# A DLRM kernel on one core: half of W1 loaded behind the first gather, and the feature units of chunks 0 and 1 dealt out anew

## The chip, the cores and the metric

One core of a Trainium2 chip runs the whole program. The metric is the device time of one execution in microseconds; lower is better.

## The reference

For each of 2048 samples there are 27 feature vectors of 128 floats and one dense vector of 128. The dot products of all 351 pairs of feature vectors, behind the dense vector, are the input of a perceptron of four ReLU layers and a last row:

```python
dots = jnp.einsum('bfd,bgd->bfg', bottom_output, bottom_output)
pairs = dots[:, _TRIL_I, _TRIL_J]
x = jnp.concatenate([bottom_mlp_output, pairs, pad], axis=1)      # 2048 x 480
for w, b in ((w0, b0), (w1, b1), (w2, b2), (w3, b3)):             # 1024, 1024, 512, 256
    x = jax.nn.relu(x @ w.T + b)
return x @ w_out.T + b_out                                        # 2048 x 1
```

All is float32. The kernel splits each operand into a high and a low part, so that one product of layers takes three matmuls.

## The kernel before, in words

**Chunks and units.** The batch is cut into 8 chunks of 256 samples (columns). The features of a chunk are handled in 16 units of 16 samples. A unit takes these steps: SP loads its rows in four DMAs (`load_rows`, L458); DVE transposes them (`turn_raw`, L921, "raw"); ACT makes the high part of the result (L805) and DVE the low one (L926), both into `xt`; PE forms the products of the features (`gram`, four matmuls of 256 columns, L688); ACT moves them to `parts` (four instructions, L817); DVE transposes the low part (L945, `low_t`) and POOL adds twice (L564, L571) into `grams`. When all 16 units of a chunk are in `grams`, SP writes them to DRAM (`spill`, L405, `blocks<-grams`) and reads them back with pairs on partitions (`gather`, L410, `pairs<-blocks`); ACT and DVE split them into `x0` (L843, L980). That is the input of the next chunk's layer 0.

**Layers.** A tile of a layer is 128 outputs by 256 columns, with K steps of three matmuls each (L726). Layers 0, 1, 2, 3 have 8, 8, 4, 2 tiles of K = 4, 8, 8, 4: 96, 192, 96 and 24 matmuls, 408 in a chunk. A finished tile is drained by ACT (L833), its high part cast by DVE (L952), its low part made by POOL (L579), and the next layer waits for that on its first tile. In layer 3 the fourth K step of both tiles, nine matmuls with what goes before it, comes last (`LAST_LAYER`), as it needs layer 2's last tile.

**Order of the work.** Every engine walks the same list of steps (`steps_of`), so its queue is fixed. Steps of other work are hooked in between the matmuls: in chunk 0 a hook every 6 matmuls (`first_hooks`), in later chunks every 18 (`hooks_of`). Hook n of a chunk's units (`unit_steps`) holds raw of unit n, the xt of unit n-1, and the gram of unit n-3; so 19 hooks do 16 units. The first five hooks of a chunk's units (`AHEAD`) are placed near the end of the chunk before the one that has the rest; with them five raws and two grams. Before: chunk 0 has all 19 hooks for the features of chunk 1 (places 11 to 37 of its hooks) and at places 49 to 61 the first five for chunk 2. Chunk 1 and the later ones have 14 hooks (every 18 matmuls, the last after 252), two empty ones, and the five for the chunk after.

**SP's queue in chunk c.** `load_mlp`, rows of chunk c+1 from unit 9, rows of units 0 to 3 of chunk c+2, spill, gather, and only then rows of units 4 to 8 of chunk c+2.

**The start.** The features of chunk 0 go another way: PE turns the rows (L647), ACT copies (L790), PE multiplies (L671), ACT moves one quarter of the result (L798) and DVE three (L935). Then the weights are turned by PE in groups of four 128x128 tiles (L642, or L621 for the small vectors), ACT makes the high part (L782, L780) and DVE the low (L912, or `ones`, L909). Groups 0 to 7 are W0, 8 the small vectors, 9 to 24 W1, 25 to 34 W2 and W3. ACT issues half of the first spill and of the first gather from its own queue; the gather stands behind group 6 (`GATHER_AFTER`) and waits there for the spill. The pair columns of x are K steps 1 to 3 of layer 0; step 0 (the dense vector) of the first six tiles is done ahead of them (`EARLY_TILES`), and W1's groups 9 on are hooked in between, one every six matmuls.

## Time and profile before

| what | value |
|---|---|
| median of 3 runs | 532.54 us (530.84 to 533.41) |
| the profiled execution, its own time | 532.41 us |
| its span | 530.6 us |
| PE busy | 501.3 us (94%) |
| ACT, DVE, POOL busy | 333.7, 289.1, 260.6 us |
| mean granted TensorE clock | 0.988 |

The profiled execution's time is its span and 1.8 us around it. The engines' busy times overlap, so they don't add up to the span. The granted clock is 1.00 at 2.4 GHz and 0.50 at 1.2 GHz.

### The profile page before, as it was taken

The numbers are of one execution on the slowest core, as the hardware profiler recorded it, in microseconds if no ns is written. First come the engines' busy times: TensorE is split into PE (matmuls) and PEld (weight loads), VectorE is DVE, ScalarE is ACT, GpSimd is POOL, SyncE is SP. The second block draws the span as 40 slices with busy tenths as digits, with TensorE's granted clock in tenths as the row PEclk, the third lists the DMA queues.
The fourth block names the chain that finished last, engine by engine and source line by source line (L and its number), as shares of the span: only waits on it lengthen the run. The fifth ranks groups of instructions, "written<-read, shape, count | busy, mean of one in ns | idle before, by whom it ended". The sixth has DMA issues, their size and how long they took to land.

```text
span 530.6 us, 13442 instructions
## 1 busy us (share of the span) xinstructions
PE 501.3 (94%) x4073; PEld 491.5 (93%) x4073; DVE 289.1 (54%) x646; ACT 333.7 (63%) x844; POOL 260.6 (49%) x467
## 2 busy tenths in 40 slices
PE   6968987799999999999999999999999999999996
PEld 6858987699999899999999999999999999999996
DVE  3764877466753576446762676356753676232101
ACT  4644799747974588737883698657873698433112
POOL 2800356424865267634864287625764387524221
PEclk9996999999999999999999999999999999999999
DMA  8997677644563566356663656266653662210000
GB/s 246 264 312 156 196 119 114 114 77 81 89 109 75 94 105 104 55 109 113 102 96 67 116 96 106 44 125 109 99 79 79 117 103 43 49 47 1 1 1 0
DMA packets 281054, 53.23 MB, mean 100 GB/s; under 512 B 265126, under 2 KB 279230, under 8 KB 281022
## 3 DMA queue, kind: packets, MB, share of 16 engines
q1 hardware_dynamic: 279090, 52.22, 51.9%
q10 hardware_dynamic: 1932, 0.61, 0.5%
q8 instruction: 17, 0.28, 0.2%
q14 instruction: 15, 0.12, 0.1%
HBM read 45.71 MB, written 7.09 MB: 99 GB/s over the span
## 4 chain that ended last, share of the span: by engine, by line
PE 66%; DMA 11%; SPq 7%; ACT 5%; POOL 4%; issue 4%; DVE 3%; POOLq 0%; DVEq 0%; ACTq 0%
PE acc L726 52%; PE gram_ps L688 8%; DMA blocks<-grams 5%; ACT parts L817 3%; SPq L410 3%; DMA early_rows<-in_r_bottom_output_dram 2%; SPq L405 2%; PE gram_ps L642 2%; DMA rows<-in_r_bottom_output_dram 2%; PE gram_ps L671 2%; POOL grams L571 1%; SPq L458 1%; POOL h_a L579 1%; POOL parts L564 1%; DMA pairs<-blocks 1%
## 5 line engine op out<-in xcount | busy, mean ns | idle before, releaser
L726 PE MATMUL acc<-h_a,w_hi 128*128 128x256 f32 x1152 | 214.4, 285 | 3.9 <-POOL h_a L579 2.6
L726 PEld LDWEIGHTS acc<-h_a,w_hi 128*128 128x128 f32 x1152 | 179.1, 192 | 6.6 <-POOL h_a L579 4.3
L817 ACT ACTIVATE parts<-gram_ps 27x216 f32<-27x216 f32 x448 | 152.9, 341 | 25.7 <-PE gram_ps L688 18.5
L833 ACT ACTIVATE h_full<-acc,small_t 128x256 f32<-128x256 f32 x172 | 81.5, 474 | 132.2 <-PE acc L726 128.7
L726 PE MATMUL acc<-h_a,w_lo 128*128 128x256 f32 x576 | 162.8, 283 | 0.0
L579 POOL TENSOR_TENSOR h_a<-h_full,h_a 128x256 fp32r<-128x256 f32 x96 | 72.2, 752 | 139.6 <-DVE h_a L952 139.6
L726 PEld LDWEIGHTS acc<-h_a,w_lo 128*128 128x128 f32 x576 | 110.3, 192 | 0.0
L726 PE MATMUL acc<-h_b,w_hi 128*128 128x256 f32 x512 | 93.9, 284 | 0.0
L726 PE MATMUL acc<-x,w_hi 128*128 128x256 f32 x480 | 90.7, 288 | 0.0
L579 POOL TENSOR_TENSOR h_b<-h_full,h_b 128x256 fp32r<-128x256 f32 x64 | 47.4, 740 | 83.1 <-DVE h_b L952 83.1
L564 POOL TENSOR_TENSOR parts<-parts 128x128 f32<-128x128 f32 x112 | 82.4, 736 | 6.1 <-ACT parts L817 5.5
L926 DVE TENSOR_TENSOR xt<-raw,xt 128x432 fp32r<-128x432 f32 x112 | 82.0, 732 | 4.2 <-ACT xt L805 4.2
L921 DVE STREAM_TRANSPOSE raw<-rows 128x512 f32<-128x512 f32 x112 | 78.4, 700 | 6.2 <-DMA rows<-in_r_bottom_output_dram 6.0
L726 PEld LDWEIGHTS acc<-h_b,w_hi 128*128 128x128 f32 x512 | 79.7, 192 | 0.0
L688 PE MATMUL gram_ps<-xt 128*128 128x256 f32 x448 | 72.9, 285 | 6.3 <-ACT parts L817 5.9
L726 PEld LDWEIGHTS acc<-x,w_hi 128*128 128x128 f32 x480 | 75.5, 194 | 1.4 <-issue 0.8
L952 DVE CAST h_a<-h_full 128x256 fp32r<-128x256 f32 x96 | 32.2, 336 | 80.1 <-ACT h_full L833 80.1
L726 PE MATMUL acc<-h_b,w_lo 128*128 128x256 f32 x256 | 72.4, 283 | 0.0
L688 PEld LDWEIGHTS gram_ps<-xt 128*128 128x128 f32 x448 | 61.6, 192 | 8.8 <-DVE xt L926 4.4
L952 DVE CAST h_b<-h_full 128x256 fp32r<-128x256 f32 x64 | 18.8, 294 | 93.2 <-ACT h_full L833 93.2
L726 PE MATMUL acc<-x,w_lo 128*128 128x256 f32 x240 | 68.3, 285 | 0.0
L805 ACT ACTIVATE xt<-raw 128x432 fp32r<-128x432 f32 x112 | 62.5, 558 | 1.8 <-DVE raw L921 1.4
(59 smaller groups left out, 439.5 us busy)
## 6 DMA issues: line engine op xcount, KB each, us to landing
rows<-in_r_bottom_output_dram SPq DMA_DIRECT2D x444, 64.0 KB, 2.1
blocks<-grams SPq DMA_DIRECT2D x30, 216.0 KB, 3.9
w_raw<-in_L_rec_w_dram SPq DMA_DIRECT2D x6, 1024.0 KB, 7.9
early_rows<-in_r_bottom_output_dram SPq DMA_DIRECT2D x12, 224.0 KB, 5.7
stage_pairs<-in_L_rec_w_dram SPq DMA_DIRECT2D x1, 1408.0 KB, 9.2
w_raw<-in_L_rec_w_dram SPq DMA_DIRECT2D x2, 512.0 KB, 8.5
mlp_rows<-r_bottom_mlp_output_dram SPq DMA_DIRECT2D x8, 128.0 KB, 2.2
pairs<-blocks SPq DMA_DIRECT2D x8, 126.0 KB
```

What stands on the lines that cost most here:

```text
L405: engine.dma_start(blocks[:, :, s * RUN:(s + 1) * RUN], grams[QUAD * s:QUAD * (s + 1)]).then_inc(spilled, 16)
L410: engine.dma_start(pairs[q % P:q % P + nf * nk, q // P], src).then_inc(gathered[q // P], 16)
L564: nc.gpsimd.tensor_tensor(hh, hh, hl, ALU.add).then_inc(sum_done, 1)
L579: nc.gpsimd.tensor_tensor(h[:, m, 1, :], h_full[:, slot % 2, :], h[:, m, 0, :].bitcast(F32), ALU.subtract).then_inc(split_done, 1)
L688: last = nc.tensor.matmul(gram_ps[:, u % GRAM_RING * GRAM_BANKS + j // 2, at:at + 2 * P], xt[:, u % XT_RING, j, 0], xt[:, u % XT_RING, j]. ...
L726: last = nc.tensor.matmul(acc_slot(c, slot), weight(wp, layer, m, k), in_tile(layer, k, xp), start=(k == 0 and n == 0), stop=(k == K_TILES ...
L805: nc.scalar.activation(xt_part(u, 0), raw_cols(u), ACT.Copy).then_inc(xt_hi_done, 1)
L817: last = nc.scalar.activation(parts[quad_of(s), u % 2, :, :, 0:FEATS], gram_found(u, s), ACT.Copy)
L833: nc.scalar.activation(h_full[:, slot % 2, :], acc_slot(c, slot), ACT.Relu, bias=small_t[:, slot:slot + 1]).then_inc(drained, 1)
L921: nc.vector.transpose(raw[:, u % RAW_RING].rearrange("p j n -> p (j n)"), rows[:, r].rearrange("p j n -> p (j n)")).then_inc(raw_turned, 1)
L926: nc.vector.tensor_tensor(xt_part(u, 1), raw_cols(u), xt_part(u, 0).bitcast(F32), ALU.subtract).then_inc(xt_done, 1)
L952: nc.vector.tensor_copy(h[:, m, 0, :], h_full[:, slot % 2, :]).then_inc(high_done, 1)
```

## The change

Six things, all of which move instructions in queues; none adds or takes away arithmetic.

1. SP loads rows 4 to 7 of W1 (two DMAs of 1 MB) behind its part of the first gather. Before, one of the two stood ahead of the spill and one between spill and gather.
2. The moving of the last two units of chunk 0 is split two quarters to two between ACT and DVE (one to three before), and each of weight groups 0 to 3 on PE waits only for the unit that had its bank.
3. `GATHER_AFTER` goes from 6 to 3: ACT's half of the gather stands behind group 3.
4. All six early K steps are done in a row, then groups 9 to 11 of W1, and only then ACT and DVE split the pairs. The memset of `xt` on DVE (L1017) is thereby ahead of groups 9 to 11.
5. Chunk 0 has only the 19 hooks for chunk 1, at places 10 to 40, each place now 18 matmuls later than before as the early steps aren't counted; W2's and W3's groups follow from place 41.
6. Chunk 1 is written out, with a hook every 15 matmuls: 19 for chunk 2, the last after 285 matmuls, and right behind them the five for chunk 3. From chunk 2 on all is as before.

```diff
--- before.py
+++ after.py
@@ -57,14 +57,14 @@
-HOOK, FIRST_HOOK = 18, 6
-GATHER_AFTER, FIRST_UNIT, LATE_HOOK = 6, 11, 38
-AHEAD, AHEAD_HOOK = 5, 49
+HOOK, SECOND_HOOK, FIRST_HOOK = 18, 15, 6
+GATHER_AFTER, W1_EARLY, FIRST_UNIT, LATE_HOOK = 3, 3, 10, 41
+AHEAD = 5
 FULL_ROWS = 112
 EARLY_SLOTS = 8
 RAW_RING = 2
 EARLY_XT = 2 * XT_RING
-EARLY_BY_ACT = 1
+EARLY_BY_ACT = [1] * (UNITS - 2) + [2] * 2
 OUT_HOOK, EARLY_TILES = 2, 6
@@ -146,43 +146,40 @@
         steps.append(("weights", n))
         if n == GATHER_AFTER:
             steps.append(("gather",))
-    return steps + [("pairs",)]
+    return steps
 def first_hooks():
-    places = [FIRST_UNIT + 2 * i for i in range(4)] + [FIRST_UNIT + 8 + 4 * i // 3 for i in range(UNIT_HOOKS - 4)]
-    hooks = [[] for _ in range(3 * sum(K_TILES[n] * M_TILES[n] for n in range(3)) // FIRST_HOOK)]
-    for n in range(BEFORE_CHUNK, LATE_WEIGHTS):
-        hooks[n - BEFORE_CHUNK].append(("weights", n))
-    for u, place in enumerate(places):
-        hooks[place] += unit_steps(u, 1)
+    hooks = [[] for _ in range(3 * TILE0[3] // FIRST_HOOK)]
+    for n in range(BEFORE_CHUNK + W1_EARLY, LATE_WEIGHTS):
+        hooks[n - BEFORE_CHUNK - W1_EARLY].append(("weights", n))
+    for u in range(UNIT_HOOKS):
+        hooks[FIRST_UNIT + 5 * u // 3] += unit_steps(u, 1)
+    assert FIRST_UNIT + 5 * (UNIT_HOOKS - 1) // 3 < LATE_HOOK
     for n in range(LATE_WEIGHTS, W_GROUPS):
         hooks[LATE_HOOK + n - LATE_WEIGHTS].append(("weights", n))
-    assert places[-1] < LATE_HOOK
-    for n in range(AHEAD):
-        hooks[AHEAD_HOOK + 3 * n] += unit_steps(n, 2)
     return hooks
-def hooks_of(now, ahead):
-
-
-
-    hooks = [unit_steps(n, 1) for n in range(AHEAD, UNIT_HOOKS)] if now else []
+def hooks_of(now, ahead, begun, every):
+
+
+
+    hooks = [unit_steps(n, 1) for n in range(begun, UNIT_HOOKS)] if now else []
     if ahead:
-        hooks += [[] for _ in range(len(hooks), 3 * TILE0[2] // HOOK)] + [unit_steps(n, 2) for n in range(AHEAD)]
+        hooks += [[] for _ in range(len(hooks), 3 * TILE0[2] // every)] + [unit_steps(n, 2) for n in range(AHEAD)]
     return hooks
-def chunk_steps(now, ahead, first):
+def chunk_steps(now, ahead, first, second):
     steps, done = [], 0
-    hooks = first_hooks() if first else hooks_of(now, ahead)
-    every = FIRST_HOOK if first else HOOK
+    every = FIRST_HOOK if first else SECOND_HOOK if second else HOOK
+    hooks = first_hooks() if first else hooks_of(now, ahead, 0 if second else AHEAD, every)
     hooks.reverse()
     def products(layer, m, k, k1):
@@ -200,8 +197,8 @@
                 steps.append(("out",))
     if first:
-        for m in range(EARLY_TILES):
-            products(0, m, 0, 1)
+        steps += [("mm", 0, m, 0, 1) for m in range(EARLY_TILES)]
+        steps += [("weights", BEFORE_CHUNK + n) for n in range(W1_EARLY)] + [("pairs", 0)]
     for layer in range(3):
         for m in range(M_TILES[layer]):
             if (layer, m) == (2, 2) and now:
@@ -209,7 +206,7 @@
             products(layer, m, 1 if first and layer == 0 and m < EARLY_TILES else 0, K_TILES[layer])
     assert not any(hooks)
     if now:
-        steps.append(("pairs",))
+        steps.append(("pairs", 1))
     steps += [("mm", 3, m, k0, k1) for m, k0, k1 in LAST_LAYER]
     return steps
@@ -218,7 +215,7 @@
     fixed = isinstance(c, int)
-    return chunk_steps(not (fixed and c == CHUNKS - 1), not (fixed and c >= CHUNKS - 2), fixed and c == 0)
+    return chunk_steps(not (fixed and c == CHUNKS - 1), not (fixed and c >= CHUNKS - 2), fixed and c == 0, fixed and c == 1)
 def dlrm_program(nc, x, x_mlp, w0, b0, w1, b1, w2, b2, w3, b3, w_out, b_out, y):
@@ -519,11 +516,12 @@
                 sp.dma_start(stage_small[r:r + m, :], src).then_inc(small_loaded, 16)
                 r += m
             sp.dma_start(bout[:, :], b_out.rearrange("(o n) -> o n", o=1)).then_inc(small_loaded, 16)
-            for i in range(3):
+            for i in range(2):
                 load_weights(1, w1, 2 * i, 2 * i + 2, w1_loaded[i])
             spill(0, (0, 1))
-            load_weights(1, w1, 6, 8, w1_loaded[3])
             gather(0, PIECES[0::2])
+            for i in range(2, 4):
+                load_weights(1, w1, 2 * i, 2 * i + 2, w1_loaded[i])
             for u in range(ROWS_RING):
                 load_rows(1, u)
             for i in range(2):
@@ -589,7 +587,8 @@
                         add_parts(c + step[1], step[2])
             chunk(0)
-            with pool.Fori(1, CHUNKS - 2) as c:
+            chunk(1)
+            with pool.Fori(2, CHUNKS - 2) as c:
                 chunk(c)
             chunk(CHUNKS - 2)
             chunk(CHUNKS - 1)
@@ -600,10 +599,10 @@
             def turn_weights(n):
                 g, bank, ring = ORDER[n], weight_bank(n), GRAM_RING * GRAM_BANKS
-                if n == 0:
-
-                    pe.wait_ge(early_moved, UNITS)
-                    pe.wait_ge(grams_done, UNITS)
+                if n < ring:
+
+                    pe.wait_ge(early_moved, UNITS + 1 - ring + n)
+                    pe.wait_ge(grams_done, UNITS + 1 - ring + n)
                 elif BEFORE_CHUNK <= n < LATE_WEIGHTS:
                     pe.wait_ge(w_done, max(n - 1, BEFORE_CHUNK))
@@ -763,7 +762,8 @@
                 elif step[0] == "mlp":
                     turn_mlp(0)
             chunk(0)
-            with pe.Fori(1, CHUNKS - 2) as c:
+            chunk(1)
+            with pe.Fori(2, CHUNKS - 2) as c:
                 chunk(c)
             chunk(CHUNKS - 2)
             chunk(CHUNKS - 1)
@@ -794,7 +794,7 @@
                 act.wait_ge(gram_done, u + 1)
                 if u == 0:
                     act.wait_ge(grams_zeroed, 1)
-                for s in range(EARLY_BY_ACT):
+                for s in range(EARLY_BY_ACT[u]):
                     last = nc.scalar.activation(gram_place(u, s), early_gram(u, s), ACT.Copy)
                 last.then_inc(early_moved, 1)
@@ -865,7 +865,7 @@
                     elif step[0] == "mlp":
                         mlp_hi(c + 1)
                     elif step[0] == "pairs":
-                        pairs_hi(c + 1)
+                        pairs_hi(c + step[1])
                     elif step[0] == "out" and not (isinstance(c, int) and c == 0):
                         out_row(c - 1)
@@ -888,10 +888,9 @@
                     weights_hi(step[1])
                 elif step[0] == "mlp":
                     mlp_hi(0)
-                elif step[0] == "pairs":
-                    pairs_hi(0)
             chunk(0)
-            with act.Fori(1, CHUNKS - 2) as c:
+            chunk(1)
+            with act.Fori(2, CHUNKS - 2) as c:
                 chunk(c)
             chunk(CHUNKS - 2)
             chunk(CHUNKS - 1)
@@ -931,7 +930,7 @@
                 dve.wait_ge(gram_done, u + 1)
                 if u == 0:
                     dve.wait_ge(grams_zeroed, 1)
-                for s in range(EARLY_BY_ACT, GROUP):
+                for s in range(EARLY_BY_ACT[u], GROUP):
                     last = nc.vector.tensor_copy(gram_place(u, s), early_gram(u, s))
                 last.then_inc(grams_done, 1)
@@ -1000,7 +999,7 @@
                     elif step[0] == "mlp":
                         mlp_lo(c + 1)
                     elif step[0] == "pairs":
-                        pairs_lo(c + 1)
+                        pairs_lo(c + step[1])
             nc.vector.memset(xt_full.rearrange("p r j (s f) -> p (r j s) f", f=QUAD)[:, :, FEATS:], 0.0).then_inc(xt_zeroed, 1)
@@ -1012,12 +1011,11 @@
                     weights_lo(step[1])
                 elif step[0] == "mlp":
                     mlp_lo(0)
-                elif step[0] == "pairs":
-                    pairs_lo(0)
             nc.vector.memset(xt[:].bitcast(F32).rearrange("p r j h (s f) -> p (r j h s) f", f=QUAD)[:, :, FEATS:],
                              0.0).then_inc(xt_zeroed, 1)
             chunk(0)
-            with dve.Fori(1, CHUNKS - 2) as c:
+            chunk(1)
+            with dve.Fori(2, CHUNKS - 2) as c:
                 chunk(c)
             chunk(CHUNKS - 2)
             chunk(CHUNKS - 1)
```

ACT's queue at the start, from the last moves of chunk 0's features to the groups behind the pairs, before and then in the change (L405 or L402 is the spill, L410 or L407 the gather, L782 a weight group, L843 the pairs):

```order
L798 ACTIVATE grams<-gram_ps 27x4x27 x3
L405 DMA blocks<-grams 864x1x64 x2
L838 ACTIVATE x<-turned_ps 128x256
L782 ACTIVATE w_hi<-gram_ps 128x512 x7
L410 DMA pairs<-blocks 56x1x256
L410 DMA pairs<-blocks 104x1x256
L782 ACTIVATE w_hi<-gram_ps 128x512
L780 ACTIVATE small_t<-gram_ps 128x24
L843 ACTIVATE x<-pairs 128x256 x3
L782 ACTIVATE w_hi<-gram_ps 128x512 x4
```

```order
L798 ACTIVATE grams<-gram_ps 27x4x27 x5
L402 DMA blocks<-grams 864x1x64 x2
L838 ACTIVATE x<-turned_ps 128x256
L782 ACTIVATE w_hi<-gram_ps 128x512 x4
L407 DMA pairs<-blocks 56x1x256
L407 DMA pairs<-blocks 104x1x256
L782 ACTIVATE w_hi<-gram_ps 128x512 x4
L780 ACTIVATE small_t<-gram_ps 128x24
L782 ACTIVATE w_hi<-gram_ps 128x512 x3
L843 ACTIVATE x<-pairs 128x256 x3
```

Three W0 groups moved from ahead of the gather to behind it, and three W1 groups from behind the pairs to ahead of them.

DVE's queue in the second half of chunk 1: first the rows of before from the last `low_t` of chunk 2's units to the first raw of chunk 3's, then the same rows of the change:

```order
L945 STREAM_TRANSPOSE low_t<-parts 128x128 x2
L951 REGISTER_ALU
L952 CAST h_b<-h_full 128x256
L951 REGISTER_ALU
L952 CAST h_b<-h_full 128x256
L918 ISA
L920 ISA
L921 STREAM_TRANSPOSE raw<-rows 128x512
```

```order
L944 STREAM_TRANSPOSE low_t<-parts 128x128 x3
L951 CAST h_b<-h_full 128x256
L920 STREAM_TRANSPOSE raw<-rows 128x512
L951 CAST h_a<-h_full 128x256
L920 STREAM_TRANSPOSE raw<-rows 128x512
```

The units for chunk 2 end later in the chunk, and the raws of chunk 3's units follow them more closely. The end of chunk 1 on DVE, in the change (before it reads the same but for the register instructions):

```order
L920 STREAM_TRANSPOSE raw<-rows 128x512
L925 TENSOR_TENSOR xt<-raw,xt 128x4x4x27
L944 STREAM_TRANSPOSE low_t<-parts 128x128
L951 CAST h_a<-h_full 128x256
L979 TENSOR_TENSOR x<-pairs,x 128x256 x3
```

The raw is that of chunk 3's unit 4; it still stands ahead of the cast of layer 2's last tile.

## Rows read from the trace of the kernel before

**Rows 1.** The page: busy us and share by engine.

```profile
PE 501.3 (94%) x4073; PEld 491.5 (93%) x4073; DVE 289.1 (54%) x646; ACT 333.7 (63%) x844; POOL 260.6 (49%) x467
```

**Rows 2.** Waits of PE: us in total, times, longest us.

```profile
PE gram_ps L688 <- ACT parts L817: 5.9, 9, 0.8
PE gram_ps L642 <- DVE ones L909: 3.8, 1, 3.8
PE acc L726 <- POOL h_a L579: 2.6, 5, 1.0
```

**Rows 3.** Timeline of DVE and SP at the start: start, us, instruction, [idle before].

```profile
27.24 3.21 DVE L935 COPY grams<-gram_ps 27x108 f32<-27x108 f32 x9 [0.30 <-PE gram_ps L671]
30.48 1.73 SPq L405 DMA_DIRECT2D blocks<-grams  x2
37.64 1.68 SPq L410 DMA_DIRECT2D pairs<-blocks  x2
```

**Rows 4.** Timeline of ACT and DVE around the first gather.

```profile
32.35 3.86 ACT L782 ACTIVATE w_hi<-gram_ps 128x512 fp32r<-128x512 f32 x7
37.64 1.91 ACTq L410 DMA_DIRECT2D pairs<-blocks  x2
32.97 4.28 DVE L912 TENSOR_TENSOR w_lo<-gram_ps,w_hi 128x512 fp32r<-128x512 f32 x7
```

**Rows 5.** Timeline of PE around the first gather.

```profile
36.97 0.28 PE L726 MATMUL acc<-x,w_lo 128*128 128x256 f32 x1
...
41.04 1.12 PE L642 MATMUL gram_ps<-ident,w_raw 128*128 128x128 f32 x4 [3.79 <-DVE ones L909]
...
47.10 0.77 PE L726 MATMUL acc<-x,w_hi 128*128 128x256 f32 x2
...
50.54 0.60 PE L642 MATMUL gram_ps<-ident,w_raw 128*128 128x128 f32 x4
```

**Rows 6.** Stretches of 0.5 us: PE, PEld, DVE, ACT, POOL busy, PEclk, DMA share, GB/s.

```profile
40.00:40.50 0.50, 0.00 (x0) 0.00 (x0) 0.27 (x1) 0.28 (x2) 0.00 (x0) 0.64 0.64 211
50.00:50.50 0.50, 0.50 (x5) 0.50 (x4) 0.25 (x1) 0.46 (x2) 0.00 (x0) 0.62 0.81 127
```

**Rows 7.** Stretch 65.4 to 99.6, with groups of ACT in 65 to 100.

```profile
65.40:99.60 34.20, 25.93 (x190) 23.49 (x190) 22.86 (x50) 30.97 (x83) 20.33 (x36) 1.00 0.72 113
...
L817 ACT ACTIVATE parts<-gram_ps 27x216 f32<-27x216 f32 x64 | 21.8, 341 | 2.2 <-POOL grams L571 1.6
L805 ACT ACTIVATE xt<-raw 128x432 fp32r<-128x432 f32 x14 | 7.9, 563 | 1.3 <-DVE raw L921 1.1
L833 ACT ACTIVATE h_full<-acc,small_t 128x256 f32<-128x256 f32 x5 | 2.4, 475 | 0.1
```

**Rows 8.** Timeline of PE: first and last gram of chunk 0's hooks (16 in all).

```profile
65.48 0.71 PE L688 MATMUL gram_ps<-xt 128*128 128x256 f32 x4 [0.23 <-issue]
...
96.08 0.71 PE L688 MATMUL gram_ps<-xt 128*128 128x256 f32 x4 [0.81 <-ACT parts L817]
```

**Rows 9.** The chain that ended last: a stretch of 18 matmuls.

```profile
134.92 2.16 PE acc L726 x18
```

**Rows 10.** The end of chunk 1, timelines of PE, SP and DVE.

```profile
163.41 0.64 PE L688 MATMUL gram_ps<-xt 128*128 128x256 f32 x4
...
184.33 0.51 PE L726 MATMUL acc<-h_a,w_hi 128*128 128x256 f32 x2 [1.02 <-POOL h_a L579]
...
185.68 0.50 PE L726 MATMUL acc<-x,w_hi 128*128 128x256 f32 x2
...
166.73 3.42 SPq L405 DMA_DIRECT2D blocks<-grams  x4
174.18 3.04 SPq L410 DMA_DIRECT2D pairs<-blocks  x4
...
181.20 0.71 DVE L921 STREAM_TRANSPOSE raw<-rows 128x512 f32<-128x512 f32 x1 [1.77 <-DMA rows<-in_r_bottom_output_dram]
```

**Rows 11.** Stretch: chunk 1 as a whole, columns as in rows 6.

```profile
127.20:185.68 58.48, 57.25 (x473) 56.54 (x472) 34.26 (x76) 40.27 (x106) 33.20 (x52) 1.00 0.51 87
```

## Prediction

> **What bounds the kernel now.** I began with the page's busy shares: PE works 501.3 of 530.6 us [rows 1], so no other engine bounds the whole, and the change, which adds no matmul, can only touch the 29 us in which PE stands, or PE's clock. The waits of PE come next [rows 2]: 3.8 us at the first gather, 5.9 us behind ACT, 2.6 us behind POOL. Each belongs to another stage, and each stage is touched.
>
> The head. PE's early matmuls end at 37.25 and it stands until 41.04; ACT had waited in its queue for the spill until 37.64, and the groups behind its gather were late. The reader should see in [rows 5, 6] that this hole costs twice: the granted clock falls to half at 40.2 while PE stands, and comes back at 50.4. The matmuls for the pairs begin at 47.10.
>
> The middle. From the first gram at 65.48 to the last at 96.08 [rows 8], PE is busy 25.93 of 34.2 us and ACT 30.97 [rows 7]: ACT bounds this stretch. A unit costs ACT four moves of 0.341 and a high part of 0.563, 1.93 us, about 1.98 as its queue runs, and a drain of 0.475 every 24 matmuls. Fifteen unit intervals took 30.6 us, 2.04 each; PE alone would need 8 matmuls of 0.12 (18 in 2.16 us, [rows 9]) and 0.48 for a gram, 1.44.
>
> The chunk's end. In chunk 1 PE waits 1.02 us at 184.33 for POOL's low part of layer 2's last tile, whose cast stood on DVE behind the raw of chunk 3's unit 4, and that waited for its rows until 181.20 [rows 10]. Those rows stand in SP's queue behind spill and gather, and the spill waits for the last unit. From the last gram (163.41) to rows in place (181.1) are 17.7 us and to the next chunk's first matmul (185.68) 22.3 us. This is a second clock beside PE's, and PE meets it with only a microsecond to spare.
>
> **The change, part by part.** *Head.* Moving two quarters each takes two of nine 0.357 us copies off DVE's last run [rows 3]: the spill is issued 0.7 us earlier, at 29.8. Chunk 1's spill lands 7.4 us after its issue with one issuer that takes 3.42 (166.73 to 174.18, when the gather goes out, [rows 10]); two issuers take 1.73 [rows 3], so 5.7 us with no weights on the way, against 7.1 now. The spill lands at 35.5 instead of 37.6. ACT issues its gather until 37.4 (1.91, [rows 4]), makes the high part of group 4 by 38.0 (3.86 / 7), DVE the low part by 38.6 (4.28 / 7), and PE goes on at about 38.7. Groups 4 to 7 before it are paced by DVE (low parts of 0 to 3 from 32.3, 0.61 each, then 0.44) and end near 35.2, so the hole is 3.5 us, not 3.8. That PE starts on the groups at 29.2 instead of 30.6 is worth nothing by itself: ACT and DVE take them later. Then twelve early matmuls, `ones` at 40.7, the memset (0.6) in DVE's idle time, six more matmuls, groups 9 and 10 (0.44 each) to 42.1, DVE's low part of 9 to 42.9, group 11, its two halves to 44.6, and pairs on ACT and DVE: PE begins on the pairs at 45.1. The gather is issued by 37.4 and hidden under this. That is 2.0 us before 47.10 with the same groups turned. The next 12 matmuls and group 12 take 1.9 us at full clock against the 3.4 us from 47.10 to 50.54 [rows 5]. Head, if the clock holds: **-3.5 us**. If it falls as now, all early matmuls double, the pairs begin at about 47.3, and the earlier return of the clock is worth about a microsecond: -0.7.
>
> The clock is a coin here: before, it fell 2.95 us into the hole after steady work [rows 5, 6]; the new hole is 3.5 us, behind groups with small gaps. I take it that it holds, at little over even odds. The Trainium skill (TensorE: Matmul & The Clock Gate, What's actually happening) says that "the default state is throttled, and activity releases the throttle"; by that rule alone this hole would throttle too, and the time be that of the second rival; the trace agrees that a hole does it, but shows one hole only.
>
> W1's last 2 MB are issued at about 37 and group 17 is needed near 50; the loads of rows behind them slip by some 3 us, with the first needed at 55 or later. Nothing, while that cover holds; if the megabytes were late PE would wait for them, and before, a MB issued at 32.3 took 10.4 us.
>
> *Middle.* The first gram comes 84 matmuls behind that point instead of 78: +0.7. Units are 10 matmuls apart instead of 8, but ACT still sets the pace: per interval it gains two matmuls' share of a drain, 0.04 us, so +0.5 over fifteen. In exchange PE is at matmul 264 at the last gram, not 228: 36 x 0.12 = -4.3. Two grams of 0.48 leave for chunk 1: -1.0. Middle: **-4.1 us**. The W2 and W3 groups and the second gather (19 us before the chunk's end, and spill and gather take some 13) stay hidden.
>
> *Chunk 1.* The last unit's gram comes after 285 matmuls and fifteen grams instead of 252 and thirteen: 33 x 0.12 + 2 x 0.48 = +4.9. What follows it is not PE's time but the 22.3 us of the chain: SP's order is untouched, and the cast of layer 2's last tile still stands behind the raw of unit 4. The two moved grams are in this. PE alone would need, from that gram on, 123 matmuls, three grams and 0.5: 16.8, so it would stand about 5.5 us where it stood 1.2 [rows 11]. At 15 matmuls apart ACT also has 1.98 + 1.25 x 0.475 = 2.57 us of work per 2.28 of PE in layer 0, and 2.27 per 2.28 in layer 1, so that a lag of about a microsecond built in layer 0 is not made good: I add 0.7 (bounds 0 and 2). And a hole of 5.5 us lets the clock fall at the start of chunk 2. Bounds: nothing, and half of the 9.4 us from 41.0 to 50.4, 4.7; the nearest row is the steady work from 46.3 to 50.4 ahead of the clock's return, half of 4.1: 2.1. Chunk 1: 4.9 + 0.7 + 2.1 = **+7.7 us**.
>
> Chunks 2 to 7 are as before: 0.
>
> **Sum.** -3.5 - 4.1 + 7.7 = +0.1, on the profiled execution's 532.41: 532.5. That execution lies 0.13 under the median of 532.54, so 532.6.
>
> **The rivals.** *The chain at chunk 1's end doesn't bind.* If spill, gather and rows pass quicker than the 17.7 us, for instance since the DMA queues are empty, the whole of +7.7 but the two grams goes: -3.5 - 4.1 + 1.0 = -6.6, 526.0. For it speaks only that PE's own work sets every other stretch; against it, that the same wait recurs chunk after chunk (five waits on POOL for h_a, [rows 2]).
>
> *Both holes throttle.* The head gives 0.7 instead of 3.5: 535.4, slower. The place is group 8 on PE; the price 2.8 us; it decides once the hole at 38 lets the clock fall. A hole of similar length did it before.
>
> *The chain binds but the clock stays.* 532.6 - 2.1 = 530.5, just inside "same".
>
> *ACT bounds chunk 1.* If at 15 apart drains come late too, PE waits in layer 0 and again at each layer's first tile, 2 us beyond my 0.7, and the chain starts as much later: 534.6, or 537 with a throttled head.
>
> *The change doesn't do what it says*: spill and gather land as before because the queues, not W1, set them. Then the head gives 1 us or less, near the second rival.
>
> **How the numbers follow.** The forecast has 0.32; the chain not binding 0.18; both holes throttling 0.22; no throttling at chunk 1's end 0.14; ACT bounding chunk 1 0.09; spill and gather as before 0.05. About 0.5% (2.7 us) can be told from no change. Faster takes the 0.18, half of the 0.14 and a little of the forecast's spread: 0.29. Slower takes half to two thirds of the second rival, half of the fourth and fifth, and some of the forecast's: 0.27. Same: 0.44. The range is 526.5 to 536.5: it leaves out the end of the first rival and the worst of the fourth; the forecast's own is 530 to 535.
>
> **What would show it.** Right: PE's matmuls on the pairs begin near 45 at a clock of 1.00; the last gram of chunk 0's hooks some 46 us after that and a chunk 1 that starts near 119.5 instead of 127.2; then a chunk 1 of about 64 us, with a wait of 5 to 6 us on POOL L579 at its end, DVE idle on rows ahead of its raw, and a clock of 0.50 in the first microseconds of chunk 2. Wrong: no wait over 2 us at chunk 1's end, a clock of 0.50 before 45 us, or waits on ACT in chunk 1's layer 0.

## The result, and the profile after

The changed kernel takes 537.43 us (median of 17 runs, 535.87 to 539.31), the kernel before beside it 533.94 us (17 runs): the ratio is 1.0072, 95% interval 1.0053 to 1.0091. It is slower by 0.7%, some 3.8 us. The prediction was 532.6 us with "same" as the likeliest case, and 537.4 lies 0.9 us outside its range. It started from the median of three runs of the kernel before, 532.54; beside the change that kernel took 1.4 us more. Of the change itself the forecast said +0.1 us, and it missed that by 3.4 to 3.7.

The profiled execution took 539.31 us, 1.9 more than its median, and the one of before 532.41, 1.5 less than the median of these 17. So the two traces differ by 6.9 us where the kernels differ by 3.5 to 3.8. Single terms are read from the traces; verdicts come from the medians.

The page of the changed kernel: span, busy time by engine, and the granted clock in 40 slices (answering to [rows 1]).

```profile
span 537.5 us, 13242 instructions
...
PE 505.3 (94%) x4073; PEld 495.7 (92%) x4073; DVE 287.0 (53%) x644; ACT 333.6 (62%) x846; POOL 261.6 (49%) x467
...
PEclk9996999899999989999999999999999999999998
```

PE is busy 4.0 us longer on the same 4073 matmuls, so part of the loss is clock; the rest of the 6.9 is standing. Its waits (us in total, times, longest; answering to [rows 2]):

```profile
PE acc L725 <- POOL h_a L577: 6.3, 5, 4.0
...
PE gram_ps L620 <- DVE w_lo L911: 4.2, 1, 4.2
PE gram_ps L687 <- ACT parts L817: 2.8, 4, 0.8
PE gram_ps L641 <- DVE w_lo L911: 2.6, 2, 2.0
PE gram_ps L641 <- ACT parts L817: 2.5, 1, 2.5
...
PE acc L725 <- DVE x L979: 1.7, 1, 1.7
```

The wait on POOL has grown from 2.6 to 6.3 us, and its longest from 1.0 to 4.0: that is chunk 1's end. The wait at the gather is 4.2 instead of 3.8. One is new: 1.7 for the pairs. The single one of 2.5 behind ACT, ahead of a weight group, was there before, 2.1 us long:

```profile
99.61 0.66 PE L642 MATMUL gram_ps<-ident,w_raw 128*128 128x128 f32 x4 [2.11 <-ACT parts L817]
```

What ACT cost the grams is down from 5.9 to 2.8.

PE's timeline around the first gather, after (answering to [rows 5]; start, us, instruction, [idle before]):

```profile
40.60 0.30 PE L620 MATMUL gram_ps<-ident,stage_small 24*128 24x24 f32 x1 [4.22 <-DVE w_lo L911]
...
44.83 1.80 PE L641 MATMUL gram_ps<-ident,w_raw 128*128 128x128 f32 x8
47.30 0.66 PE L641 MATMUL gram_ps<-ident,w_raw 128*128 128x128 f32 x4 [0.67 <-DVE w_lo L911]
49.70 0.72 PE L725 MATMUL acc<-x,w_hi 128*128 128x256 f32 x2 [1.74 <-DVE x L979]
```

and ACT's and SP's of the same place (answering to [rows 3, 4]):

```profile
30.84 3.33 SPq L402 DMA_DIRECT2D blocks<-grams  x2
37.26 1.91 ACTq L407 DMA_DIRECT2D pairs<-blocks  x2
39.22 2.06 ACT L782 ACTIVATE w_hi<-gram_ps 128x512 fp32r<-128x512 f32 x4 [4.61 <-issue]
45.92 0.60 ACT L782 ACTIVATE w_hi<-gram_ps 128x512 fp32r<-128x512 f32 x1 [4.55 <-PE gram_ps L641]
48.00 0.60 ACT L782 ACTIVATE w_hi<-gram_ps 128x512 fp32r<-128x512 f32 x1 [0.72 <-PE gram_ps L641]
48.49 1.02 ACT L843 ACTIVATE x<-pairs 128x256 fp32r<-128x256 f32 x3
```

The spill landed 6.4 us after its issue, where 5.7 were expected and it took 7.1 before. The matmuls on the pairs begin at 49.70, 2.6 later than before and 4.6 later than forecast. The pairs themselves were long there (the last piece landed at 44.4, and ACT splits all three without a wait); what came late is group 11, which stands ahead of them.

Stretches of 2 us, columns as in [rows 6]:

```profile
38.00:40.00 2.00, 0.00 (x0) 0.00 (x0) 0.15 (x1) 0.78 (x2) 0.00 (x0) 0.89 0.28 75
40.00:42.00 2.00, 1.40 (x6) 1.35 (x7) 2.00 (x4) 1.37 (x4) 0.00 (x0) 0.50 0.77 189
...
50.00:52.00 2.00, 2.00 (x11) 2.00 (x11) 0.32 (x1) 0.00 (x0) 0.00 (x0) 0.50 0.77 120
...
104.00:106.00 2.00, 2.00 (x14) 2.00 (x12) 0.69 (x1) 0.60 (x1) 1.18 (x3) 0.61 0.00 0
106.00:108.00 2.00, 2.00 (x13) 2.00 (x11) 0.69 (x1) 0.60 (x1) 0.00 (x0) 0.54 0.66 145
```

The clock (third number from the end) fell in the hole before 40.6, as before, and then twice where it had not: behind the wait for the pairs, and behind the 2.5 us at 103.6, a wait that had left it at full before. Chunk 2's start at half clock is a third (the fifteenth slice of the page). Then the middle and chunk 1's end on PE and SP (answering to [rows 8, 10]):

```profile
68.75 0.71 PE L687 MATMUL gram_ps<-xt 128*128 128x256 f32 x4
...
99.75 0.71 PE L687 MATMUL gram_ps<-xt 128*128 128x256 f32 x4
...
103.64 0.66 PE L641 MATMUL gram_ps<-ident,w_raw 128*128 128x128 f32 x4 [2.46 <-ACT parts L817]
...
105.16 1.05 PE L641 MATMUL gram_ps<-ident,w_raw 128*128 128x128 f32 x4
...
168.46 0.64 PE L687 MATMUL gram_ps<-xt 128*128 128x256 f32 x4
...
171.69 4.63 SPq L402 DMA_DIRECT2D blocks<-grams  x4
178.59 3.06 SPq L407 DMA_DIRECT2D pairs<-blocks  x4
181.93 10.85 SPq L455 DMA_DIRECT2D rows<-in_r_bottom_output_dram  x20
...
188.62 0.50 PE L725 MATMUL acc<-h_a,w_hi 128*128 128x256 f32 x2 [4.01 <-POOL h_a L577]
```

and DVE's there, with the raw of unit 4 ahead of the cast that PE waits for:

```profile
185.50 0.71 DVE L920 STREAM_TRANSPOSE raw<-rows 128x512 f32<-128x512 f32 x1 [5.21 <-DMA rows<-in_r_bottom_output_dram]
...
186.85 0.25 DVE L951 CAST h_a<-h_full 128x256 fp32r<-128x256 f32 x1
```

From the last gram to the next chunk are 21.4 us (168.46 to 189.89), before 22.3. Chunks 1, 2 and 3 as stretches (columns as in [rows 6], the first number after the colon being the length; chunk 1 of before began at 126.52, not at the 127.20 that [rows 11] start from, and took 59.2):

```profile
126.75:189.89 63.14, 58.72 (x486) 58.10 (x485) 39.13 (x87) 45.50 (x119) 34.59 (x54) 1.00 0.61 103
189.89:250.69 60.80, 59.54 (x478) 58.69 (x477) 33.89 (x77) 40.60 (x107) 33.31 (x52) 0.97 0.55 94
250.69:309.41 58.72, 58.02 (x477) 57.21 (x477) 34.69 (x77) 40.72 (x107) 33.01 (x52) 1.00 0.56 95
```

The sum of the two traces: PE turns the dense rows, with which the start ends, 1.0 later (29.84 against 28.83; this place lies anywhere from 28.6 to 31.0 in the twenty traces, with either head); from there to the first matmul on pairs +1.6; from there to the first gram +0.7; first to last gram +0.4; from there to chunk 1 -3.4; chunk 1 +4.0; chunk 2 (60.80 against 58.53) +2.3; the rest +0.4. Together 7.0.

### The profile page after: what moved, and what is told of

It reads as the page before. It is cut to its first block, busy times and chain, and to the rows that moved or that the text cites. A ratio compares the mean times of both kernels' runs of the same rounds, so it can differ in the third digit from the quotient of the medians.

```text
span 537.5 us, 13242 instructions
## 1 busy us (share of the span) xinstructions
PE 505.3 (94%) x4073; PEld 495.7 (92%) x4073; DVE 287.0 (53%) x644; ACT 333.6 (62%) x846; POOL 261.6 (49%) x467
## 4 chain that ended last, share of the span: by engine, by line
PE 69%; DMA 9%; SPq 6%; issue 4%; POOL 4%; ACT 4%; DVE 2%; ACTq 0%; POOLq 0%; DVEq 0%
PE acc L725 54%; PE gram_ps L687 8%; DMA blocks<-grams 5%; ACT parts L817 3%; SPq L407 3%; DMA early_rows<-in_r_bottom_output_dram 2%; PE gram_ps L641 2%; SPq L402 2%; PE gram_ps L670 2%; DMA rows<-in_r_bottom_output_dram 2%; POOL h_a L577 1%; POOL grams L569 1%; POOL parts L562 1%; SPq L455 1%; PE turned_ps L646 1%
## 5 line engine op out<-in xcount | busy, mean ns | idle before, releaser
L725 PE MATMUL acc<-x,w_hi 128*128 128x256 f32 x480 | 92.7, 292 | 1.8 <-DVE x L979 1.7
L920 DVE STREAM_TRANSPOSE raw<-rows 128x512 f32<-128x512 f32 x112 | 78.4, 700 | 10.5 <-DMA rows<-in_r_bottom_output_dram 10.2
L725 PEld LDWEIGHTS acc<-x,w_hi 128*128 128x128 f32 x480 | 77.0, 198 | 3.4 <-DVE x L979 2.0
L951 DVE CAST h_a<-h_full 128x256 fp32r<-128x256 f32 x96 | 30.8, 321 | 81.9 <-ACT h_full L833 81.6
```

Source lines behind the costliest of these rows:

```text
L725: last = nc.tensor.matmul(acc_slot(c, slot), weight(wp, layer, m, k), in_tile(layer, k, xp), start=(k == 0 and n == 0), stop=(k == K_TILES ...
L920: nc.vector.transpose(raw[:, u % RAW_RING].rearrange("p j n -> p (j n)"), rows[:, r].rearrange("p j n -> p (j n)")).then_inc(raw_turned, 1)
L951: nc.vector.tensor_copy(h[:, m, 0, :], h_full[:, slot % 2, :]).then_inc(high_done, 1)
```

## The experiments

"Head" is everything up to the matmuls on pairs and the clock they run at, "tail" the end of chunk 1. Theory A: the head costs 1.5 to 2.5 us, since three W0 groups stand behind the gather and the clock falls, and the tail the rest. Theory B: the whole loss is chunk 1's tail, where unit 4's rows of the next chunk stand in SP's queue behind the late spill and gather; the new unit places would gain without it. Every ratio is against the kernel before, run between on the same chip, with its 95% interval. Five groups of kernels were run.

### The two halves alone, and the tail's chain taken away

**head_only**: the changed head with the units' places and the loop of before.

```diff
-GATHER_AFTER, W1_EARLY, FIRST_UNIT, LATE_HOOK = 3, 3, 10, 41
-AHEAD = 5
+GATHER_AFTER, W1_EARLY, FIRST_UNIT, LATE_HOOK = 3, 3, 8, 35
+AHEAD, AHEAD_HOOK = 5, 46
...
+    for n in range(AHEAD):
+        hooks[AHEAD_HOOK + 3 * n] += unit_steps(n, 2)
...
-            chunk(1)
-            with pe.Fori(2, CHUNKS - 2) as c:
+            with pe.Fori(1, CHUNKS - 2) as c:
```

> The head of the change alone (W1 behind the gather, gather behind group 3, groups 9 to 11 ahead of the pairs, two quarters each for the last units), with the units of chunks 0 and 1 and the loop as before. Theory A (the head costs, since three W0 groups stand behind the gather and PE's hole lets the clock fall): 1.5 to 2.5 us slower than before, matmuls on the pairs from about 49. Theory B (the whole loss is the end of chunk 1): within 0.7 us of before. By my prediction of the head: 3.5 us faster.

Measured: 534.68 us, 1.0019 (0.9981 to 1.0056). The head gives nothing; at best 1 us, at worst 3 lost. In its trace the pairs begin at 48.11, 18.1 us behind the spill's issue (before 16.6, after 18.9), although the clock was back at full by 44.

**units_only**: the head of before with the new places for the units.

```diff
-HOOK, FIRST_HOOK = 18, 6
-GATHER_AFTER, FIRST_UNIT, LATE_HOOK = 6, 11, 38
-AHEAD, AHEAD_HOOK = 5, 49
+HOOK, SECOND_HOOK, FIRST_HOOK = 18, 15, 6
+GATHER_AFTER, FIRST_UNIT, LATE_HOOK = 6, 13, 44
+AHEAD = 5
...
+    places = [FIRST_UNIT + 5 * u // 3 for u in range(UNIT_HOOKS)]
...
+            chunk(1)
+            with pe.Fori(2, CHUNKS - 2) as c:
```

> The new places of the units in chunks 0 and 1 alone, with the head as before. Theory A: 1 to 2.5 us slower than before: chunk 1 some 4.7 us longer with a wait of about 4 us on POOL at its end, and half-speed matmuls at the start of chunk 2, against 4 to 5 us gained in chunk 0. Theory B: the whole 3.5 us of the change.

Measured: 537.99 us, 1.0081 (1.0044 to 1.0118). The whole loss is here, as theory B had it (the change beside it: 537.43). Chunk 1 takes 63.8 us with a wait of 3.92 on POOL at its end, chunk 2 60.0.

**after_rows4**: the changed kernel with unit 4's rows ahead of the gather in SP's queue. They need the place of unit 0's rows, which is free when the raw of unit 0 is done, well before.

```diff
                 spill(c + 1)
+                early = ROWS_RING + 1 if more and not start else ROWS_RING
+                for u in range(ROWS_RING, early):
+                    load_rows(c + 2, u)
                 gather(c + 1)
                 if more:
-                    for u in range(ROWS_RING, ROWS_RING + AHEAD):
+                    for u in range(early, ROWS_RING + AHEAD):
                         load_rows(c + 2, u)
```

> The changed kernel, but in chunks 1 to 6 SP issues the rows of unit 4 of chunk c+2 between spill and gather, so that the raw of unit 4 no longer waits for the gather's issue. If the chain spill, gather, rows sets chunk 1's end: the wait of 4 us there shrinks to what spill, gather and pairs themselves cost, and the 1 us wait at the end of chunks 2 to 6 goes: 5 to 8 us faster than the changed kernel. If the gather or the pairs are what is late: within 1 us of the changed kernel.

Measured: 532.34 us, 0.9964 (0.9936 to 0.9991): 5 to 6 us under the changed kernel. SP's and DVE's timelines at chunk 1's end:

```profile
169.35 4.50 SPq L402 DMA_DIRECT2D blocks<-grams  x4
174.12 2.39 SPq L455 DMA_DIRECT2D rows<-in_r_bottom_output_dram  x4
176.65 3.08 SPq L407 DMA_DIRECT2D pairs<-blocks  x4
...
178.08 0.71 DVE L923 STREAM_TRANSPOSE raw<-rows 128x512 f32<-128x512 f32 x1
```

The four loads go out in the time in which SP waits for the spill to land. The raw follows its cast without a wait, PE's wait of 4.0 us is gone, chunk 1 takes 59.28 and chunk 2 58.67. So the chain over unit 4's rows is what made the tail long.

**before_rows4**: the same edit on the kernel before.

> The kernel before with the same move of unit 4's rows ahead of the gather in chunks 1 to 6. If the wait of 1 us per chunk is that chain: 4 to 7 us faster than before, chunks 57.3 us long instead of 58.5. If something else is late next: less than 2 us.

Measured: 531.74 us, 0.9967 (0.9937 to 0.9996), some 2 us where 4 to 7 were expected. In the trace only chunk 1's wait went, from 1.02 to 0.38 us; chunks 2 to 6 keep the 0.38 on POOL that they had. So the rows' chain bound chunk 1 alone, and what makes the 0.38 was not looked for.

### What the clock costs, and the new unit places without the tail

**units_rows4**: `units_only` with the edit of `after_rows4`.

> The head of before, the new places of the units in chunks 0 and 1, and unit 4's rows ahead of the gather in chunks 1 to 6. If the head of the change costs about 0.7 us by itself: 531 to 531.5 where the changed head with the same move gave 532.3, some 3 us under before. If the changed head is a gain that its clock hides: above 532.5.

Measured: 530.02 us, 0.9916 (0.9882 to 0.995). Without the tail the new places gain 4.5 us, and the head of before beats the changed head (532.34) by 2.3 us.

**after_warm_tail**: the changed kernel with 24 extra matmuls in the hole at chunk 1's end.

```diff
+                if isinstance(c, int) and c == 1 and (layer, m, k0) == (3, 0, 3):
+                    pe.wait_ge(out_drained, c)
+                    for _ in range(24):
+                        nc.tensor.matmul(turned_ps[:, 1, 0:CHUNK], weight(w_hi, 3, 0, 0), in_tile(3, 0, 0), start=True, stop=True)
```

> The changed kernel with 24 more matmuls of 0.12 us on PE in the 4 us wait at chunk 1's end; their product is not used. If that wait costs a second time through the clock: chunk 2 takes 58.6 us instead of 60.8, 2 us faster than the changed kernel, with the wait's end where it was. If the length of chunk 2 comes from late rows or pairs: no change.

Measured: 537.23 us, 1.0045 (1.0012 to 1.0078). Its trace has chunk 1 as long (63.19) and chunk 2 at 59.26 instead of 60.80: the fallen clock costs chunk 2 1.5 us where 2.1 were set. By the medians this kernel is 0.2 us under the changed one, by the ratios 1.4, with intervals that overlap; so 1.5 stands on one trace each.

**rows4_warm_head**: `after_rows4` with 32 extra transposes in the head's hole.

```diff
+                    if n == 2 * ring:
+                        for _ in range(32):
+                            nc.tensor.transpose(acc[:, 1, 0:P], ident[:], ident[:])
```

> The changed kernel with unit 4's rows ahead of the gather, and 32 transposes of the identity on PE ahead of group 8, in the hole at the first gather; their result is not used. My prediction's head with the clock kept: PE begins on the pairs near 46 to 47 instead of 48 to 49.7, and 2 to 3.5 us come off the 532.3. If the weights' chain on ACT and DVE sets the head and not the clock: within 1 us of 532.3.

Measured: 531.18 us, 0.9946 (0.9915 to 0.9977), about a microsecond under `after_rows4`, with overlapping intervals. PE there:

```profile
41.85 0.24 PE L625 MATMUL gram_ps<-ident,stage_small 24*128 24x24 f32 x1
...
44.26 1.04 PE L646 MATMUL gram_ps<-ident,w_raw 128*128 128x128 f32 x8
46.27 0.66 PE L646 MATMUL gram_ps<-ident,w_raw 128*128 128x128 f32 x4 [0.97 <-DVE w_lo L916]
48.67 0.53 PE L730 MATMUL acc<-x,w_hi 128*128 128x256 f32 x2 [1.74 <-DVE x L984]
```

The clock is full from 38.8 to 49.0. From the end of the hole to the pairs are 6.8 us, where the change took 9.1 and the forecast had 6.4 (38.7 to 45.1); so the clock explains most of what was too long in this stretch. The time gained by it is small all the same: the extra transposes ran until 41.9 and may have held up group 8, and the clock fell again at 49.0, behind the wait of 1.74.

**head_gather6**: `head_only` with `GATHER_AFTER` 6.

```diff
-GATHER_AFTER, W1_EARLY, FIRST_UNIT, LATE_HOOK = 3, 3, 8, 35
+GATHER_AFTER, W1_EARLY, FIRST_UNIT, LATE_HOOK = 6, 3, 8, 35
```

> The head of the change alone, but ACT's half of the gather stands behind group 6 as before. If the three W0 groups behind the gather are what the head costs: 1 to 2 us faster than the head alone (534.7) and at or below before. If the early run of groups 9 to 11 ahead of the pairs costs: as the head alone or slower.

Measured: 535.8 us, 1.0021 (0.9983 to 1.006), while its trace shows the earliest pairs of all, 45.41 (the forecast's own 45.1), and took 532.03. The other runs went from 533.0 to 539.6, at clocks of 0.980 to 0.992. One trace is one draw.

### Spreading the units, and which part of the head

**spread_ahead0**: the kernel before, only its units further apart; chunk 0 keeps the units of chunk 2.

```diff
-GATHER_AFTER, FIRST_UNIT, LATE_HOOK = 6, 11, 38
-AHEAD, AHEAD_HOOK = 5, 49
+GATHER_AFTER, FIRST_UNIT, LATE_HOOK = 6, 13, 44
+AHEAD, AHEAD_HOOK = 5, 51
...
-    places = [FIRST_UNIT + 2 * i for i in range(4)] + [FIRST_UNIT + 8 + 4 * i // 3 for i in range(UNIT_HOOKS - 4)]
+    places = [FIRST_UNIT + 5 * u // 3 for u in range(UNIT_HOOKS)]
```

> The head of before, chunk 0's units 10 matmuls apart as in the change, but the five hooks for chunk 2 kept at chunk 0's end, and chunk 1 in the loop as before. If the units of chunk 2 moved into chunk 1 are what costs, and the wider spread in chunk 0 is the gain: chunk 0 some 3 us shorter, chunk 1 58.5 to 59, in all 2 to 3.5 us faster than before. If the spread gives nothing once the rest stays: within 0.7 us of before.

Measured: 531.46 us, 0.9941 (0.9907 to 0.9976).

**spread_rows4**: that with unit 4's rows ahead of the gather.

> The same with unit 4's rows ahead of the gather in chunks 1 to 6. Before, this move alone gave 1.7 us at most (0.3%): so 0.5 to 1.5 us faster than the spread alone, near 530, level with the changed units and this move (530.0).

Measured: 530.38 us, 0.9918 (0.9886 to 0.9951), what `units_rows4` gives too. Once the tail is mended, no difference shows between the two chunks that may run the five units; spreading chunk 0's is the gain.

**rows4_gather6**: `after_rows4` with `GATHER_AFTER` 6.

> The changed kernel with unit 4's rows ahead of the gather and ACT's half of the first gather behind group 6 again. If the three W0 groups behind the gather cost the changed head its 2.3 us (532.3 against 530.0 with the old head): 530 to 530.7. If groups 9 to 11 ahead of the pairs cost them: 532 to 533.

Measured: 530.01 us, 0.9917 (0.9887 to 0.9948), some 2 us under `after_rows4` on another chip. ACT's timeline:

```profile
45.63 0.71 ACT L846 ACTIVATE x<-pairs 128x256 fp32r<-128x256 f32 x2
...
49.73 0.42 ACT L846 ACTIVATE x<-pairs 128x256 fp32r<-128x256 f32 x1 [3.39 <-DMA pairs<-blocks]
```

The pairs come sooner (46.84 on PE), but the gather's last piece lands 12.2 us after the gather's first issue at 37.51 and 10.2 after ACT issued that piece itself, and PE waits 2.21 us for it.

**units_rows4_w1**: `units_rows4` with half of W1 behind the gather, and nothing else of the head.

```diff
-            for i in range(3):
+            for i in range(2):
                 load_weights(1, w1, 2 * i, 2 * i + 2, w1_loaded[i])
             spill(0, (0, 1))
-            load_weights(1, w1, 6, 8, w1_loaded[3])
             gather(0, PIECES[0::2])
+            for i in range(2, 4):
+                load_weights(1, w1, 2 * i, 2 * i + 2, w1_loaded[i])
```

> Head of before but for the two megabytes of W1 issued behind the gather; new places of the units; unit 4's rows ahead of the gather. If W1 on the DMA queues delayed the spill, the spill lands 1 us sooner and the time is 529 to 529.7; if the spill's own packets set its landing: 529.7 to 530.5, as without the move.

Measured: 532.92 us, 0.9973 (0.9946 to 1.0), 2.9 over `units_rows4`. ACT's timeline:

```profile
42.23 0.42 ACT L847 ACTIVATE x<-pairs 128x256 fp32r<-128x256 f32 x1 [0.97 <-DMA pairs<-blocks]
44.93 0.42 ACT L847 ACTIVATE x<-pairs 128x256 fp32r<-128x256 f32 x1 [2.28 <-DMA pairs<-blocks]
46.95 0.42 ACT L847 ACTIVATE x<-pairs 128x256 fp32r<-128x256 f32 x1 [1.60 <-DMA pairs<-blocks]
```

The gather went out at 38.62, so its last piece took 8.3 us. In the eleven traces with W1 in front it took 5.9 to 8.0 (middle value 7.0), in the nine with W1 behind 7.1 to 9.0 and once 12.2 (middle value 8.0). The spill landed 6.2 us after its issue; with W1 in front it took 6.3 to 7.1, once 8.5 (middle value 6.6), with W1 behind 6.2 to 6.4. On the old head the move costs more than it gives. That the slower gather is the cause fits, but it rests on one trace.

### The head's parts apart, on one chip

**units_rows4_again** and **after_rows4_again** are the kernels of those names once more, as the pair to compare with.

> The same kernel as units_rows4, for a comparison on this chip: 529.5 to 530.5.

> The same kernel as after_rows4, beside the one with the old head. If the changed head costs time: 1.5 to 3 us more than with the old head. If that difference came from the batch: within 1 us of it.

Measured: 530.18 us, 0.9918 (0.9886 to 0.995), and 531.68 us, 0.9964 (0.9939 to 0.9988). The changed head costs 1.5 us against the old one, 2.3 in the first such pair; in each pair the intervals overlap a little. With the tail unmended no such cost shows (537.43 for the change, 537.99 for `units_only`). So the changed head costs between nothing and some 2.5 us, and gains in none of the pairs beyond the noise.

**units_rows4_gather3**: the old head but for the gather behind group 3.

```diff
-GATHER_AFTER, FIRST_UNIT, LATE_HOOK = 6, 13, 44
+GATHER_AFTER, FIRST_UNIT, LATE_HOOK = 3, 13, 44
```

> As units_rows4, but ACT's half of the gather behind group 3; W1's loads, the moves and groups 9 to 11 as before. If the three W0 groups behind the gather are what the changed head costs: 1.5 to 2.5 us more than units_rows4. If it is W1's megabytes beside the gather: within 1 us of it.

Measured: 528.46 us, 0.9902 (0.9868 to 0.9935). The three W0 groups behind the gather cost nothing here; whether they gain over `units_rows4_again` (0.9918) the intervals don't tell. ACT's timeline:

```profile
44.71 0.42 ACT L846 ACTIVATE x<-pairs 128x256 fp32r<-128x256 f32 x1 [1.72 <-DMA pairs<-blocks]
45.35 0.89 ACT L846 ACTIVATE x<-pairs 128x256 fp32r<-128x256 f32 x2 [0.23 <-DMA pairs<-blocks]
46.15 0.58 ACT L785 ACTIVATE w_hi<-gram_ps 128x512 fp32r<-128x512 f32 x1
```

and PE's:

```profile
46.26 1.05 PE L644 MATMUL gram_ps<-ident,w_raw 128*128 128x128 f32 x4
...
48.12 0.60 PE L644 MATMUL gram_ps<-ident,w_raw 128*128 128x128 f32 x4
48.47 0.48 PE L728 MATMUL acc<-x,w_hi 128*128 128x256 f32 x2
```

Here three W1 groups are turned before the pairs too, but between the early matmuls, and ACT splits the pairs as they land, before the groups. PE reaches the pairs 16.2 us behind the spill's issue and doesn't wait for them; the three groups in a row of the change made PE stand 0.67 and 1.74 us. The old order has its own price: ACT waits for the gather ahead of the groups, and in the other nine traces with this order PE stood 0.3 to 3.0 us ahead of group 11.

**rows4_gather6_w1old**: `rows4_gather6` with W1 loaded as before.

```diff
-            for i in range(2):
+            for i in range(3):
                 load_weights(1, w1, 2 * i, 2 * i + 2, w1_loaded[i])
             spill(0, (0, 1))
+            load_weights(1, w1, 6, 8, w1_loaded[3])
             gather(0, PIECES[0::2])
-            for i in range(2, 4):
-                load_weights(1, w1, 2 * i, 2 * i + 2, w1_loaded[i])
```

> As rows4_gather6, with W1 loaded ahead of and between spill and gather as before. Its gather landed 12 us after its issue with the 2 MB behind it. If these hold up ACT's pieces of the gather: the last piece lands within 7.5 us of the issue, and 528 to 529.5, the fastest of all. If not: as rows4_gather6, 530.

Measured: 529.86 us, 0.9934 (0.9909 to 0.9959), beside 530.01 for `rows4_gather6` on another chip. The gather's last piece landed 6.1 us after the first issue, as expected of W1 in front, and yet the time is the same: the late piece of the other trace doesn't show in the medians.

### The last pair

**after_rows4_w1old**: `after_rows4` with W1 loaded as before. **best_again**: `units_rows4_gather3` once more.

> The changed kernel with unit 4's rows ahead of the gather, and W1's loads as before; the gather behind group 3 and groups 9 to 11 ahead of the pairs as in the change. If W1's 2 MB behind the gather are what the changed head costs: 529 to 530 where it was 531.7 and 532.3 with them, as groups 9 to 11 then have the gather's landing hidden. If the order of the groups costs: 531 to 532.5.

> The same kernel as units_rows4_gather3, run again: 528.5 to 530 if its 528.46 holds, still over 0.7% faster than before; above 530 if that was the batch.

Measured: 532.13 us, 0.9983 (0.9962 to 1.0004), and 529.43 us, 0.992 (0.9891 to 0.9949). W1 back in its old place mends nothing in the changed head. It is `after_rows4_w1old` that stands beside `best_again` on one chip with the same W1 loads, the same `GATHER_AFTER` and the same tail: what differs is how the early steps, groups 9 to 11 and the pairs are ordered, and how the moves of the last two units are shared; together they cost 2.7 us. In the two traces, which differ by 2.8 us, the clock was at half for 17.1 us and for 10.2 us ahead of the program's end; at half speed PE does half the work, so up to 3.4 us of the difference can be clock. PE of `after_rows4_w1old`:

```profile
49.68 0.79 PE L727 MATMUL acc<-x,w_hi 128*128 128x256 f32 x2 [1.74 <-DVE x L981]
```

19.1 us behind the spill's issue, against 17.2 in `best_again`. With the gather behind group 6 the same order cost nothing (529.86 beside 530.18 on one chip). The traces show a reason. From the turning of the dense rows to the first matmul on pairs the ten traces with the old order took 17.9 to 19.0 us. The new order took 18.1 to 20.1 with the gather behind group 3 (seven traces) and 16.0 to 16.7 with it behind group 6 (three traces). Behind group 3, group 8 and all eighteen early matmuls come after the hole at the gather; behind group 6, group 8 and twelve of them can run before it. Why these earlier pairs don't make the kernel faster than the old order stays open, as does why `head_gather6`, which has them too, measured 535.8.

`units_rows4_gather3` beats both kernels: 528.46 and 529.43 us in two groups of runs, 0.8 to 1.0% under the kernel before and 1.5 to 1.7% under the changed one by the ratios (0.9902 and 0.992 over 1.0072). It keeps two of the change's ideas, the new unit places and the gather behind group 3, and adds the four row loads ahead of the gather.

## Why the prediction was wrong

**Chunk 1: right in mechanism and place, a little too dear.** The last gram came 41.7 us into the chunk instead of 36.9 (+4.8, forecast +4.9). The chain behind it took 21.4 us, not an unchanged 22.3. The lag of ACT, put at 0.7, was nothing: PE's only wait of note in the chunk ahead of its end is 0.41 us. The clock fell at chunk 2's start, and the chunk lost 2.3, of which `after_warm_tail` gives the clock 1.5. Together +6.3 for a forecast of +7.7. That rows in SP's queue do it is shown by `after_rows4`, where four loads, moved, return 5 to 6 us. The rival "the chain doesn't bind" is dead.

**Middle: -4.1 forecast, -2.3 in the trace.** Grams at 10 matmuls apart and the 84 matmuls came as counted (+0.4 and +0.7, forecast +0.5 and +0.7). Behind the last gram -3.4 stood where -5.3 was expected. The wait ahead of a W2 group took 2.46 us instead of 2.11, and behind it the clock was at half from 104.4 to 107.8, where groups took 1.05 us instead of 0.60: half of those 3.4 us, 1.7, and the 0.35 are about the missing 1.9 us. The wait stood in the trace of before, and no rival priced a fall of the clock there. It is a second coin: of the twenty traces all have this wait, of 2.1 to 2.5 us, and in eleven the clock fell in it or behind it. `spread_ahead0` shows the gain itself, 0.6%.

**Head: this step failed.** Of "-3.5 us" nothing came: +2.6 in the trace, 1.0 of it the later start, which the change doesn't explain, and between -1 and +3 in the medians (`head_only`). The forecast had the pairs 15.3 us behind the spill's issue (29.8 to 45.1), the trace 18.9. Term by term:

- The spill's issue, "0.7 us earlier": right. It went out 1.00 us after the turning of the dense rows, before 1.65.
- Spill landing 5.7 us after its issue: 6.4. The sum took two issuers as 1.7 us faster than one and gave W1 the rest. By the middle values of the traces W1's megabytes in front were worth 0.2 us.
- "I take it that it holds": the clock fell at 39.6 in the hole, which was 4.2 us long where 3.5 were put, and came back at 46.4. From the end of the hole to the pairs 9.1 us passed instead of 6.4. With the clock kept they were 6.8 (`rows4_warm_head`), so by that one trace 2.3 of the 2.7 are clock and 0.4 the chain of groups 9 to 11. The standing of PE ahead of group 11 and ahead of the pairs, 0.67 and 1.74 us, was in the working (42.1 to 42.9, and behind group 11 to 45.1); the 1.74 came in all ten traces with this order.
- The earlier return of the clock, worth 1.5 behind the pairs: 0. It fell again at 49.8, behind the 1.74 us, as in seven of these ten traces.
- "Nothing" for W1 behind the gather: I had asked who waits for W1, not what W1 delays. The gather beside it landed about 1 us later (middle values). The changed head hid this behind its groups, so it is no part of the measured loss.

So the step is the head's two clock terms, 2.3 and 1.5 us, and the spill's 0.7. The second rival had the first fall, at 0.22 too low: its +2.8 is 0.7 to 1.0 short of the measured loss. But the clock isn't all of it: with it kept through the hole, the changed kernel with the mended tail gained only about 1 us (`rows4_warm_head`), within the noise.

**Range and chances.** With the head at the measured nothing, the forecast's other terms give 536.1, inside the range; with the +2.6 of the trace 538.7, outside it. That 537.4 lies outside is in part luck: 1.4 us of it came with the median of before that the sum was set on, and the measured loss on 532.6 would be 536.1 to 536.4. Two misses also nearly cancelled, the middle's gain 1.8 us smaller and chunk 1's cost 1.4 smaller than forecast. The range leaned on a head that gains in every case: even the worst rival let it give something. The sign of a rearrangement whose parts all wait on one another deserved a rival with a loss.

## What to carry over

When work that other queues wait for is moved later, follow every chain behind it (here: last unit, spill, gather, rows, raw, cast, low part, next layer), and put a load that is ready ahead of an instruction that will wait. When a transfer is moved off one critical transfer, ask which it now lies beside. And compare medians for the verdict, since an execution's clock moves it by more than such a change.

## What the runs showed of the hardware

- The last piece of the first gather, in pieces of 1 KB on ACT's queue, landed 5.9 to 8.0 us after the gather's first issue with W1 issued ahead of it (eleven traces), and 7.1 to 9.0 with 2 MB of W1 from SP's queue behind it (eight traces). In the ninth such trace, `rows4_gather6`, it took 12.2. Only there was the piece issued behind W1's first megabyte (39.48 against 39.23); it landed at 49.7, after that one (48.5) and before the second (51.5). The Trainium skill (DMA: Bandwidth & Descriptors, Queues, rings and completion order) says that an engine "round-robins between the queue rows it has work for" a packet at a time. No run here can show it; the one slow trace doesn't tell taking turns from waiting behind a megabyte, and nobody varied that order.
- The clock fell after a wait of 2.46 us that followed busy work, and stayed at half for some 3 to 4 us; the same wait, of 2.1 to 2.5 us, left it at full in nine of twenty traces. The wait of 1.74 us ahead of the pairs let it stand in three of ten traces, `head_only` among them. The rule of the Trainium skill quoted in the prediction gives the direction, and the trace agrees with it in the 4.2 us hole, where I had bet on full clock. Which holes it fell in differed between executions: one kernel's runs lay up to 8 us apart (`head_only`, 531.97 to 539.82, at clocks of 0.995 and 0.979), while `units_rows4_gather3` kept within 2.5 in seven runs.
- The first two spill DMAs occupied SP's queue for 1.4 to 1.8 us in thirteen traces and for 3.2 to 3.8 in seven (the change's 3.33 at 30.84); what decides it was not tried.
